# A graph-network layer on Trainium2: TensorE's sums moved one quarter earlier, VectorE's additions moved to the head of a group, the maximum taken on VectorE, the end reordered

## The chip, the cores and the metric

One core of one Trainium2 chip runs the kernel. The metric is the device time of one execution in microseconds (us). The kernel before took 2541.52 us, the median of 3 runs (2540.87 to 2542.66). The execution that was profiled took 2545.81 us by its own time and has a span of 2544.0 us.

## The reference

The layer works on a graph with 6250 nodes (64 numbers each) and 206250 edges (32 numbers each), sorted by the node they end in (`dst`).

```python
h = jnp.maximum(_layernorm(x, axis=-1), 0.0)
msg_in = jnp.concatenate([h[src], h[dst], edge_attr_32], axis=-1)
messages = act(msg_in @ W1 + b1) @ W2 + b2            # act = swish
att_logits = act(msg_in @ Wa1 + ba1) @ Wa2 + ba2
att = jax.nn.softmax(att_logits, axis=0)              # over all edges
aggregated = jax.ops.segment_sum(messages * att, dst, num_segments=6250)
upd_in = jnp.concatenate([h, aggregated], axis=-1)
out = x + act(upd_in @ Wu1 + bu1) @ Wu2 + bu2
```

All of it is float32. Each edge needs one row that depends on its source, one that depends on its destination, and its own features, through two small layers; then a softmax over all edges, and a sum by destination.

## The kernel before

A first stage (about 100 us) normalises x and writes two tables to HBM: `p_tab` with h @ [W1, Wa1] for sources and `q_tab` with the same for destinations, 128 numbers a node.

The main stage goes through 81 groups of 20 tiles of 128 edges (the last, LAST = 80, has 12). A quarter is 4 tiles; a full group has NQ = 5 of them, one PSUM bank (`ps_z[q]`, 128x512) each. All loops over groups are written out in full, so each engine has one long fixed order of instructions, and engines meet only at semaphores.

For group g and quarter q:

- GpSimd (`gather`, L388 to L397) fetches the source rows of each tile from `p_tab` with one indirect DMA of 64 KB (128 rows of 512 bytes) into `p_rows[:, a, ...]`, where a = g % 2. So a quarter's place in `p_rows` is free for group g when VectorE has added the same quarter of group g - 2: `pool.wait_ge(z_ok, (g - 2) * NQ + q + 1)`.
- ScalarE (`one_hot_abs`, `one_hot_relu`) makes the one-hot matrix of the destinations in `comb`, from `dst_b`, which SyncE loads (`load_dst_b`, 960 KB a group). SyncE also loads the edge features into `comb` (`load_ef`) and the window of `q_tab` (`load_window`), when `z_done` says that TensorE has read the group that had that place.
- TensorE (`zmm`, L604 to L615) computes z, the sum before the first activation without the source part, for group g + 1 while VectorE works on group g, and counts `z_done` once a quarter. In the trace each float32 matmul stands as two instructions, so a quarter is 8 of them (128x128).
- VectorE (`add_rows`, L893 to L897) adds the gathered source rows to the quarter in PSUM, and counts `z_ok`. ScalarE (L516) applies Silu into `s2` and counts `silu_ok`, which also frees the bank for the next z.
- VectorE (`logits`, L884 and L886) forms the attention logits, L944 and L946 add the bias and take the largest of each lane. TensorE turns that column into a row (`column_max`, L633), VectorE takes the largest (`group_max`, L904), TensorE spreads it to all lanes (`spread_max`, L638), and VectorE (`running_max`, L915) writes `neg_max`.
- ScalarE (`weights`, L504 and L506) takes the exponentials, VectorE (`one_hots` L861, `weighted` L890 and L891) makes `hot` and `v`, TensorE (`sums`, L617 to L625) sums v by destination into `ps_part` with 20 matmuls (40 instructions, 128x96), and counts `part_done`. VectorE (`add_part`, L869 to L876) loads the window's first node into a register, waits for `part_done` and adds the sums to `acc`; then it updates `ref` and `zp`.

The order inside one group g on TensorE is `column_max(g-1)`, z quarter 0 of g + 1, `spread_max(g-1)`, z quarters 1 and 2, `sums(g-1)`, z quarters 3 and 4. On VectorE it is: the additions of quarters 1 to 4 of group g between the other steps, then L944 and L946, then quarter 0 of group g + 1, then `add_part(g-1)`:

```python
if nxt is not None:
    add_rows(nxt, 1 - a, 0)
if late:
    add_part(g - 1, 1 - a)
```

The end (from L986 on) takes the last maximum, the last weights and sums, adds them, reads a flag and branches on it (a general path that isn't taken here), and computes the update of all nodes in 7 blocks (`rescale`, `aggregate`, `own_part`, `new_rows`, `whole_y`).

## Time and profile before

| what | value |
|---|---|
| median of 3 runs | 2541.52 us |
| the profiled execution, own time | 2545.81 us |
| its span | 2544.0 us |
| GpSimd busy | 1529.6 us, 60% of the span, 1628 instructions |
| TensorE matmuls busy | 1335.2 us, 52%, 7010 instructions |
| VectorE busy | 953.6 us, 37%, 1722 instructions |
| ScalarE busy | 925.1 us, 36%, 1106 instructions |
| mean granted TensorE clock | 0.653 |
| DMA | 228.42 MB, mean 90 GB/s |

Busy time is the time with an instruction at work. "Idle before" in a row is the time that the engine stood still before the instruction, and the name behind the arrow is what ended it, as the semaphores' records tell: "issue" means that nothing recorded ended it, "remote" that the semaphore's releaser on this core had been done long before. Matmul records can be missing here and there.

### The profile page before, as it was taken

Reading aid. Unit: us, or ns where it says so; the run is one execution under the profiler, and the core shown is the slowest. Engines: PE = TensorE matmul, PEld = TensorE weight load, DVE = VectorE, ACT = ScalarE, POOL = GpSimd, SP = SyncE. Lnnn points to the kernel's source line nnn. Section 1 sums busy time; section 2 is a strip of 40 time slices with the busy share of each in tenths; the row PEclk is TensorE's granted clock in tenths of the full one; section 3 lists DMA queues with packets and bytes.
Section 4 is the critical chain, followed back from the end, with each engine's and each line's share of the span. In section 5 each row is a group of like instructions: output and inputs, shape, how many; then the busy total and the mean of one; then the engine's idle time right before and its main releaser. Section 6 shows DMA issues by size and latency. Waiting matters only on the chain.

```text
span 2544.0 us, 20784 instructions
## 1 busy us (share of the span) xinstructions
PE 1335.2 (52%) x7010; PEld 1126.5 (44%) x7010; DVE 953.6 (37%) x1722; ACT 925.1 (36%) x1106; POOL 1529.6 (60%) x1628
## 2 busy tenths in 40 slices
PE   5245555555455555555455555555555455555556
PEld 3234444444444444444444444444444444444444
DVE  4234334433333333433333333333333333443345
ACT  3333333433333333343333333343333333333333
POOL 3665656666666656666666666666666665666650
PEclk8666666666766666666766666666766666666667
DMA  7433333333333333333333333333333333333321
GB/s 193 105 88 84 88 85 91 87 88 92 97 88 87 87 85 90 88 88 89 98 90 88 87 86 89 89 87 87 97 93 88 88 87 85 91 87 87 95 67 27
DMA packets 101988, 228.42 MB, mean 90 GB/s; under 512 B 45185, under 2 KB 65461, under 8 KB 91637
## 3 DMA queue, kind: packets, MB, share of 16 engines
q1 hardware_dynamic: 47588, 120.63, 18.2%
q0 software_dynamic: 51584, 105.75, 16.3%
q8 instruction: 58, 0.95, 0.2%
q10 hardware_dynamic: 2704, 0.66, 0.1%
q14 instruction: 54, 0.43, 0.1%
HBM read 218.91 MB, written 8.00 MB: 89 GB/s over the span
## 4 chain that ended last, share of the span: by engine, by line
another core or an unknown queue 53%; ACT 17%; DVE 14%; issue 11%; PE 3%; DVEq 1%; ACTq 0%; SPq 0%; DMA 0%
ACT s L516 5%; DVE bank L897 5%; ACT L516 4%; ACT comb L484 3%; DVE prod L884 3%; ACT comb L490 3%; DVE lg L886 3%; PE bank L624 1%; ACT bank L504 1%; PE bank L613 1%; DVE lgb L944 1%; PE bank L575 1%; DVE gmax L904 1%; ACT fade L506 1%
## 5 line engine op out<-in xcount | busy, mean ns | idle before, releaser
L396 POOL DMA_INDIRECT p_rows<-p_tab,src_all x1612 | 1521.6, 944 | 943.7 <-issue 466.9
L613 PE MATMUL bank<-q_win,comb 128*128 128x128 f32 x3224 | 825.6, 385 | 842.6 <-issue 832.1
L613 PEld LDWEIGHTS bank<-q_win,comb 128*128 128x128 f32 x3224 | 669.0, 279 | 952.2 <-issue 950.9
L516 ACT ACTIVATE s<-bank 128x512 f32<-128x512 f32 x403 | 239.0, 594 | 1434.4 <-DVE bank L897 1424.7
L874 DVE SCALAR_TENSOR_TENSOR acc<-acc,fade,bank 65x96 f32 x80 | 24.8, 310 | 1330.3 <-remote 1326.7
L624 PE MATMUL bank<-hot,v 128*65 128x96 f32 x3224 | 393.7, 300 | 165.2 <-issue 149.7
L624 PEld LDWEIGHTS bank<-hot,v 128*65 128x65 f32 x3224 | 378.4, 180 | 186.0 <-issue 169.0
L897 DVE TENSOR_TENSOR bank<-bank,p_rows 128x512 f32<-128x512 f32 x403 | 277.0, 688 | 15.7 <-issue 15.7
L484 ACT ACTIVATE comb<-dst_b,row_of 96x1024 f32<-96x1024 int32 (+1 forms) x162 | 217.8, 1345 | 55.3 <-DMA dst_b<-dst_row 55.3
L490 ACT ACTIVATE comb<-comb,ones 96x1024 f32<-96x1024 f32 (+1 forms) x162 | 218.8, 1351 | 2.7
L861 DVE TENSOR_TENSOR hot<-bank,rel 128x960 f32<-128x960 f32 x162 | 185.1, 1143 | 0.0
L884 DVE TENSOR_TENSOR prod<-s,bank 128x512 f32<-128x512 f32 (+2 forms) x163 | 130.9, 803 | 134.4 <-ACT s L516 128.3
L886 DVE TENSOR_REDUCE lg<-prod 128x8 f32<-128x512 f32 (+2 forms) x163 | 132.4, 812 | 5.6
L504 ACT ACT_TABLE_LOAD x81 | 103.9, 1283 | 75.7 <-issue 64.4
L891 DVE TENSOR_TENSOR v<-s,bank 128x1300 f32<-128x1300 f32 x80 | 119.9, 1499 | 0.0
L516 ACT ACT_TABLE_LOAD x81 | 103.9, 1283 | 1.4
L633 PE MATMUL bank<-ident,pmax 128*1 128x128 f32 x81 | 29.8, 368 | 99.7 <-issue 96.7
L638 PE MATMUL bank<-gmax,ones 1*128 1x1 f32 x162 | 46.7, 355 | 42.2 <-DVE gmax L904 41.2
L638 PEld LDWEIGHTS bank<-gmax,ones 1*128 1x128 f32 x162 | 39.8, 303 | 64.6 <-DVE gmax L904 64.5
L633 PEld LDWEIGHTS bank<-ident,pmax 128*1 128x1 f32 x81 | 6.4, 79 | 135.3 <-issue 131.5
L904 DVE TENSOR_REDUCE gmax<-bank 1x1 f32<-1x128 f32 x81 | 21.8, 269 | 16.8 <-remote 16.3
L504 ACT ACTIVATE bank<-lgb,neg_max 128x20 f32<-128x20 f32 (+1 forms) x81 | 22.7, 281 | 1.0
(107 smaller groups left out, 321.0 us busy)
## 6 DMA issues: line engine op xcount, KB each, us to landing
dst_b<-dst_row SPq DMA_DIRECT2D x80, 960.0 KB
p_rows<-p_tab,src_all POOLq DMA_INDIRECT x1612
comb<-efT SPq DMA_DIRECT2D x80, 320.0 KB
q_win<-q_tab SPq DMA_DIRECT2D x81, 48.0 KB
p_tab<-s SPq DMA_DIRECT2D x12, 256.0 KB
q_tab<-s SPq DMA_DIRECT2D x12, 256.0 KB
out<-s SPq DMA_DIRECT2D x6, 256.0 KB, 2.3
x_sb<-x SPq DMA_DIRECT2D x2, 512.0 KB, 5.0
```

The costliest lines, as they stand in the source:

```text
L396: pool.indirect_dma_start(p_rows[:, a, t * H2:(t + 1) * H2], None, p_tab, bass.IndirectOffsetOnAxis(src_all[:, g * TG + t:g * TG + t + 1], ...
L484: nc.scalar.activation(comb[0:WIN, a, c0:c1], dst_b[:, c0:c1], ACT.Abs, bias=row_of[0:WIN, bass.ds(g, 1)]).then_inc(abs_ok, 1)
L490: nc.scalar.activation(comb[0:WIN, a, c0:c1], comb[0:WIN, a, c0:c1], ACT.Relu, scale=-1.0, bias=ones[0:WIN, 0:1]).then_inc(comb_ok, 1)
L504: nc.scalar.activation(ps_w[:, 0:tiles(g)], lgb[:, 0:tiles(g)], ACT.Exp, bias=nm).then_inc(w_ok, 1)
L516: nc.scalar.activation(silu_rows(a, q), halves(ps_z[q][:]), ACT.Silu).then_inc(silu_ok, 1)
L613: last = nc.tensor.matmul(ps_z[q][:, (t % TQ) * H2:(t % TQ + 1) * H2], comb[:, a, t * P:(t + 1) * P], q_win[:, a, :], start=True, stop=True)
L624: last = nc.tensor.matmul(ps_part[0:U1, 0:WIN], v[:, t, :], hot[:, t * WIN:(t + 1) * WIN], start=(t == 0), stop=(t == T - 1))
L861: nc.vector.tensor_tensor(hot[:, t0 * WIN:(t0 + n) * WIN].rearrange("p (t n) -> p t n", t=n), iota_c[:, 0:WIN].unsqueeze(1).broadcast_to([ ...
L884: nc.vector.tensor_tensor(prod[:, 0:t1 - t0], att, wa2c.unsqueeze(1).broadcast_to([P, t1 - t0, U]), ALU.mult).then_inc(s_sem, 1)
L886: nc.vector.tensor_reduce(lg[:, t0:t1], prod[:, 0:t1 - t0], AX.X, ALU.add).then_inc(s_sem, 1)
L891: return nc.vector.tensor_tensor(v[:, 0:T, :], s2[:, ab, 0:T, 0:U1], ps_w[:, 0:T].unsqueeze(2).broadcast_to([P, T, U1]), ALU.mult)
L897: nc.vector.tensor_tensor(ps_z[q][:], ps_z[q][:], p_rows[:, a, q * 512:(q + 1) * 512], ALU.add).then_inc(z_ok, 1)
```

## The change

- GpSimd's `gather` waits, for quarter 2, first for a new semaphore `tile_ok` (one tile's place is free), issues one gather, and waits for the rest of the quarter before the second.
- `add_rows` adds quarter 2 in two instructions, 128x128 and 128x384, and counts `tile_ok` after the first.
- On VectorE, a group begins with the additions of its quarters 0, 1 and 2, with short steps of the group before in between; the additions of quarters 3 and 4 follow the maximum and the first logits; `add_part` of group g - 2, the one-hots and the weighting of g - 1 stand at the group's end.
- The maximum over lanes no longer goes through TensorE: the biased logits of 4 blocks of 32 lanes are written side by side on 32 lanes (`biased`), reduced (`lane_max`), transposed on VectorE and reduced again (`spread_max`), and written to the 4 blocks of `neg_max`.
- On TensorE, `sums(g-1)` stands behind z quarters 0 and 1 of group g + 1, and quarters 2, 3 and 4 behind it; `column_max` and `spread_max` are gone. The one transpose that they did for the flag in group 1 goes into `sums`.
- At the end: ScalarE runs one Exp on a dummy before the last weights; VectorE makes v before it sums the weights; the wait for the last sums and the last addition to `acc` come behind the branch; five of the seven `own_part` products stand ahead of the last sums, each in a bank of its own.

```diff
@@ gpsimd, gather
-                    if not (isinstance(g, int) and g < 2):
-                        pool.wait_ge(z_ok, (g - 2) * NQ + q + 1)
+                    if g > 1:
+                        if q == 2:
+                            pool.wait_ge(tile_ok, g - 1)
+                        else:
+                            pool.wait_ge(z_ok, (g - 2) * NQ + q + 1)
                     for t in range(q * TQ, (q + 1) * TQ):
+                        if g > 1 and t == 2 * TQ + 1:
+                            pool.wait_ge(z_ok, (g - 2) * NQ + q + 1)
@@ scalar
             groups(act, group)
+            nc.scalar.activation(rz[:], ones[:, 0:1], ACT.Exp)
             weights(LAST, 0)
@@ tensor, group
-                if late:
-                    column_max(g - 1)
                 for q in [q for q in (0,) if q in quarters]:
                     zmm(nxt, 1 - a, q)
-                if late:
-                    spread_max(g - 1)
-                for q in [q for q in (1, 2) if q in quarters]:
+                for q in [q for q in (1,) if q in quarters]:
                     zmm(nxt, 1 - a, q)
                 if late:
                     sums(g - 1)
-                for q in [q for q in (3, 4) if q in quarters]:
+                for q in [q for q in (2, 3, 4) if q in quarters]:
                     zmm(nxt, 1 - a, q)
@@ tensor, end
             own_part(0)
             own_part(1)
-            column_max(LAST)
-            spread_max(LAST)
-            pe.wait_ge(zp_ok, 1)
             pe.wait_ge(silu_ok, LAST * NQ + TL // TQ)
-            nc.tensor.matmul(ps_zall, ones[:], zp[:], start=True, stop=True).then_inc(zall_done, 1)
-            sums(LAST)
+            for b in range(2, 5):
+                own_part(b)
...
@@ vector, add_rows
-                nc.vector.tensor_tensor(ps_z[q][:], ps_z[q][:], p_rows[:, a, q * 512:(q + 1) * 512], ALU.add).then_inc(z_ok, 1)
+                n = 0
+                if q == 2:
+                    n = H2
+                    nc.vector.tensor_tensor(ps_z[q][:, 0:n], ps_z[q][:, 0:n], p_rows[:, a, q * 512:q * 512 + n], ALU.add).then_inc(tile_ok, 1)
+                nc.vector.tensor_tensor(ps_z[q][:, n:], ps_z[q][:, n:], p_rows[:, a, q * 512 + n:(q + 1) * 512], ALU.add).then_inc(z_ok, 1)
@@ vector, group (new)
+                late = g > 0
+                add_rows(g, a, 0)
+                if late:
+                    logits(1 - a, 2, NQ, silu_ok, g * NQ, s_ok, g * 4 - 2)
+                add_rows(g, a, 1)
+                if late:
+                    biased(g - 1)
+                add_rows(g, a, 2)
+                if late:
+                    lane_max(g - 1)
+                    spread_max(g - 1)
+                    running_max(g - 1)
+                logits(a, 0, 2, silu_ok, g * NQ + 2, s_ok, g * 4)
+                if g < LAST - 1:
+                    add_rows(g, a, 3)
+                    add_rows(g, a, 4)
+                if g > 1:
+                    add_part(g - 2, a)
+                if late:
+                    one_hots(g - 1, 0)
+                    one_hots(g - 1, 1)
+                    weighted(g - 1, 1 - a)
...
@@ vector, end
-            dve.wait_ge(part_done, NG)
-            win = acc[:, bass.ds(node, WIN)]
-            nc.vector.scalar_tensor_tensor(win, win, fade[0:U1, 0:1], ps_part[0:U1, 0:WIN], ALU.mult, ALU.add).then_inc(acc_ok, 1)
-            dve.wait_ge(acc_ok, NG)
 
             misfit = dve.value_load(flag[0:1, 0:1], min_val=0, max_val=1)
...
+            dve.wait_ge(part_done, NG)
+            win = acc[:, bass.ds(node, WIN)]
+            nc.vector.scalar_tensor_tensor(win, win, fade[0:U1, 0:1], ps_part[0:U1, 0:WIN], ALU.mult, ALU.add).then_inc(acc_ok, 1)
+            dve.wait_ge(acc_ok, NG)
```

What this makes of the written-out orders follows for two engines. On TensorE, one group in the middle of the program, before (the z matmuls are L613, the sums L624):

```order
L633 MATMUL bank<-ident,pmax 1x128
L613 MATMUL bank<-q_win,comb 128x128 x4
L638 MATMUL bank<-gmax,ones 128x1
L613 MATMUL bank<-q_win,comb 128x128 x8
L624 MATMUL bank<-hot,v 65x96 x20
L613 MATMUL bank<-q_win,comb 128x128 x8
```

and now (z is L622, the sums L636):

```order
L636 MATMUL bank<-hot,v 65x96 x20
L622 MATMUL bank<-q_win,comb 128x128 x20
L636 MATMUL bank<-hot,v 65x96 x20
L622 MATMUL bank<-q_win,comb 128x128 x20
```

Of the next group's 20 z matmuls, 12 stood ahead of the sums and 8 behind them; now 8 stand ahead and 12 (quarters 2, 3 and 4) behind. The two small products for the maximum are gone.

On VectorE, before, from the last step of a group's logits to the second addition of the next (L897 are additions of z, L874 the addition of the sums):

```order
L886 TENSOR_REDUCE lg<-prod 128x12
L944 TENSOR_SCALAR lgb<-lg,ba2c 128x20
L946 TENSOR_REDUCE pmax<-lgb 128x1
L897 TENSOR_TENSOR bank<-bank,p_rows 128x512
L871 TENSOR_LOAD base_i
L871 ISA x2
L874 ISA
L874 SCALAR_TENSOR_TENSOR acc<-acc,fade,bank 65x96
L867 REGISTER_ALU
L867 TENSOR_SCALAR ref<-ones,neg_max 65x96
L876 SCALAR_TENSOR_TENSOR zp<-zp,fade,wsum 128x1
L897 TENSOR_TENSOR bank<-bank,p_rows 128x512
```

and now the head of a group, up to its fourth addition (L911 and L912 are additions of z):

```order
L912 TENSOR_TENSOR bank0<-bank0,p_rows 128x512
L895 TENSOR_TENSOR prod<-s2,bank7 128x768
L897 TENSOR_REDUCE lg<-prod 128x12
L912 TENSOR_TENSOR bank1<-bank1,p_rows 128x512
L918 TENSOR_SCALAR lgb<-lg,ba2c 128x20
L921 TENSOR_SCALAR lgb<-lg,ba2c 32x20 x3
L911 TENSOR_TENSOR bank2<-bank2,p_rows 128x128
L912 TENSOR_TENSOR bank2<-bank2,p_rows 128x384
L927 TENSOR_REDUCE qmax<-lgb 32x1
L932 STREAM_TRANSPOSE qmaxB<-qmax 32x32
L934 TENSOR_REDUCE top<-qmaxB 32x1
```

No wait for the sums (L871, L874) stands between the additions of quarters 0, 1 and 2 any more; it comes behind all five.

## Rows read from the trace of the kernel before

**Rows 1.** Page, three groups; list of waits: engine, line, releaser: us, times, longest.

```profile
L396 POOL DMA_INDIRECT p_rows<-p_tab,src_all x1612 | 1521.6, 944 | 943.7 <-issue 466.9
...
L861 DVE TENSOR_TENSOR hot<-bank,rel 128x960 f32<-128x960 f32 x162 | 185.1, 1143 | 0.0
...
L891 DVE TENSOR_TENSOR v<-s,bank 128x1300 f32<-128x1300 f32 x80 | 119.9, 1499 | 0.0
...
DVE acc L874 <- remote: 1326.7, 77, 17.4
...
POOL p_rows L396 <- issue: 466.9, 1532, 0.3
POOL p_rows L396 <- DVE bank L897: 439.6, 79, 8.9
```

**Rows 2.** Timeline of one group: start us, duration, engine, line, [idle before].

```profile
1227.38 0.94 POOL L396 DMA_INDIRECT p_rows<-p_tab,src_all  x1 [5.41 <-DVE bank L897]
...
1233.55 3.52 PE L624 MATMUL bank<-hot,v 128*65 128x96 f32 x40 [1.91 <-issue]
...
1237.64 0.23 DVE L944 TENSOR_SCALAR lgb<-lg,ba2c 128x20 f32<-128x20 f32 x1
...
1251.11 0.94 POOL L396 DMA_INDIRECT p_rows<-p_tab,src_all  x1 [0.30 <-issue]
...
1256.00 0.31 DVE L874 SCALAR_TENSOR_TENSOR acc<-acc,fade,bank 65x96 f32 x1 [17.31 <-remote]
1256.06 0.31 SPq L276 DMA_DIRECT2D comb<-efT  x1
...
1256.54 0.69 DVE L897 TENSOR_TENSOR bank<-bank,p_rows 128x512 f32<-128x512 f32 x1
...
1257.50 0.94 POOL L396 DMA_INDIRECT p_rows<-p_tab,src_all  x1 [5.45 <-DVE bank L897]
```

**Rows 3.** Timeline of TensorE's matmuls in the same group.

```profile
1236.90 0.75 PE L613 MATMUL bank<-q_win,comb 128*128 128x128 f32 x5
...
1241.00 0.37 PE L613 MATMUL bank<-q_win,comb 128*128 128x128 f32 x1 [0.47 <-issue]
1241.69 0.37 PE L613 MATMUL bank<-q_win,comb 128*128 128x128 f32 x1 [0.33 <-issue]
...
1255.77 1.44 PE L613 MATMUL bank<-q_win,comb 128*128 128x128 f32 x6 [0.33 <-issue]
```

**Rows 4.** Timeline of the first groups: the gathers that end GpSimd's stops.

```profile
103.76 0.94 POOL L396 DMA_INDIRECT p_rows<-p_tab,src_all  x1 [7.38 <-DVE bank L897]
143.91 0.94 POOL L396 DMA_INDIRECT p_rows<-p_tab,src_all  x1 [5.50 <-DVE bank L897]
168.34 0.94 POOL L396 DMA_INDIRECT p_rows<-p_tab,src_all  x1 [4.76 <-DVE bank L897]
```

**Rows 5.** Timeline of the first groups: VectorE after long waits, and one burst of sums.

```profile
142.76 0.28 DVE L904 TENSOR_REDUCE gmax<-bank 1x1 f32<-1x128 f32 x1 [16.26 <-remote]
...
149.30 5.33 PE L624 MATMUL bank<-hot,v 128*65 128x96 f32 x40 [1.91 <-issue]
...
166.84 0.31 DVE L874 SCALAR_TENSOR_TENSOR acc<-acc,fade,bank 65x96 f32 x1 [12.43 <-remote]
```

**Rows 6.** Timeline where the gathers end: the last gather, the last sums beside it, VectorE.

```profile
2470.55 5.24 PE L624 MATMUL bank<-hot,v 128*65 128x96 f32 x40 [1.91 <-issue]
...
2473.12 0.95 POOL L396 DMA_INDIRECT p_rows<-p_tab,src_all  x1 [0.30 <-issue]
...
2476.21 0.31 DVE L874 SCALAR_TENSOR_TENSOR acc<-acc,fade,bank 65x96 f32 x1 [0.52 <-PE bank L624]
```

**Rows 7.** Timeline: a 128x128 addition in the first stage; two places of the program's end.

```profile
77.33 0.29 DVE L795 TENSOR_TENSOR s<-bank,b_q 128x128 f32<-128x128 f32 x1 [4.87 <-issue]
...
2506.26 1.28 ACT L504 ACT_TABLE_LOAD   x1 [3.08 <-DVE neg_max L915]
...
2517.82 3.49 DVE L1079 TENSOR_TENSOR acc<-acc,ref 65x1024 f32<-65x1024 f32 x3 [3.63 <-issue]
```

More of the change, by code:

```diff
@@ L666, in _ @@
             own_part(1)
-            column_max(LAST)
-            spread_max(LAST)
-            pe.wait_ge(zp_ok, 1)
             pe.wait_ge(silu_ok, LAST * NQ + TL // TQ)
-            nc.tensor.matmul(ps_zall, ones[:], zp[:], start=True, stop=True).then_inc(zall_done, 1)
-            sums(LAST)
+            for b in range(2, 5):
+                own_part(b)
+            pe.wait_ge(acc_ok, LAST)
+            pe.wait_ge(v_ok, NG)
+            for t in range(TL):
+                if t in (0, TL // 2):
+                    pe.wait_ge(hot_ok, 2 * LAST + 1 + 2 * t // TL)
+                if t == TL // 2 + 2:
+                    pe.wait_ge(zp_ok, 1)
+                    nc.tensor.matmul(ps_zall, ones[:], zp[:], start=True, stop=True).then_inc(zall_done, 1)
+                last = nc.tensor.matmul(ps_part[0:U1, 0:WIN], v[:, t, :], hot[:, t * WIN:(t + 1) * WIN], start=(t == 0), stop=(t == TL - 1))
+            last.then_inc(part_done, 1)
             pe.wait_ge(flag_ok, 1)
@@ new lines, in running_max @@
+            def running_max(g):
+                dve.wait_ge(top_ok, g + 1)
+                wait(dve, negm_ok, 4 * g)
+                for k in range(4):
+                    nm = neg_max[32 * k:32 * (k + 1), bass.ds(g, 1)]
+                    if g == 0:
+                        nc.vector.tensor_scalar(nm, top[:], -1.0, None, ALU.mult).then_inc(negm_ok, 1)
+                    else:
+                        nc.vector.scalar_tensor_tensor(nm, top[:], -1.0, neg_max[0:32, bass.ds(g - 1, 1)], ALU.mult, ALU.min).then_inc(negm_ok, 1)
```

159 lines of the change are left out of this document (74 added, 85 removed).

## The prediction

> **What bounds the kernel now.** The page comes first: GpSimd has the largest busy share, 1521.6 us in 1612 gathers of 944 ns [rows 1]. The chain of waits is of little use here, since over half of it goes to "another core or an unknown queue". The list of waits tells more: between gathers GpSimd idles 0.30 us each time, and 79 times, 439.6 us in all, it waits for VectorE's addition [rows 1]. VectorE itself waits 1326.7 us in 77 pieces before the addition of the sums (L874), with "remote" as the releaser [rows 1].
>
> The timeline of one group shows how these hang together [rows 2]. GpSimd starts at 1227.38 and issues 20 gathers, the last at 1251.11: 23.73 us for 19 steps, 1.25 us each, and it ends at 1252.05. Then it lacks the place of a quarter 1. That addition (L897 at 1256.54) stands behind `add_part` in VectorE's order, and `add_part` waits from 1238.69 to 1256.00. GpSimd goes on at 1257.50. The group takes 30.12 us, 25.0 of gathers and 5.1 of stop.
>
> Why does `add_part` wait until 1256.00? By its records TensorE ended the sums at 1237.07 [rows 2]. But SyncE, which waits for another TensorE count (`z_done`), is released at 1256.06, in the same moment. And TensorE, with nothing to wait for, is slow in just this stretch: after a first quick run the matmuls come at 0.70 us steps, until at 1255.77 six run in 1.44 us [rows 3]. I read this so: **while gathers run, TensorE's counts are held back once some number of its matmuls have been issued, and they all come out a few us after the last gather.** The first groups bear it out. With 28 gathers (103.76 to 138.41) VectorE's wait for the maximum, also a TensorE count but with no register load ahead of it, ends at 142.76, 4.35 us after GpSimd's stop; with 16 gathers (143.91 to 163.58) L874 starts 3.26 us after it [rows 4, 5]; with 20 it is 3.95 us [rows 2]. Where gathers end at 2474.07 for good, L874 waits only 0.52 us and starts at 2476.21, with the sums over at 2475.79 [rows 6]. So GpSimd and VectorE wait for each other: the count comes only when GpSimd stands, and GpSimd stands until VectorE has the count.
>
> **The change part by part.** The stop is made of three pieces [rows 2]: 3.95 us from the last gather's end to VectorE's release, 1.23 us of VectorE (L874, two short steps, the 128x512 addition, 1256.00 to 1257.23), and 0.27 us to GpSimd's start, 5.45 us in all.
>
> *Where the stop lies now.* VectorE adds quarters 0 and 1 of a group before it needs a late TensorE count; quarter 2 stands behind 40 instructions of sums and 8 of z on TensorE. The sums began 6.2 us after GpSimd's start (1233.55); now a second addition (0.69), `add_part`'s own steps (0.54) and the maximum on VectorE (some 1.3) stand ahead of them too, so they begin at about 8.7 us. The count of quarter 2 is then given at about 15 us, later than that of the sums before (9.7 us), and is held back just the same. I expect one stop per group, again after 20 gathers, at `tile_ok`.
>
> *The second piece.* It becomes one addition of 128x128 from PSUM, 0.29 us by the nearest row [rows 7]. That is 0.94 us less. The other part of quarter 2 (about 0.56 us) is done before the first gather of 1.25 us ends, so it costs GpSimd nothing, and neither does `add_part`, which now stands behind all five additions.
>
> *The first piece.* Measured: 3.26, 3.95 and 4.35 us, longer with more gathers. What counts may be the gathers since the stop, which stay 20 (then 3.95 us), or the time since the burst of TensorE work began. That burst begins at 8.7 us, not at 6.2, which brings it from 18.5 to 16.0 us before the last gather's end; in the 16-gather stop it was 14.3 us (from 149.30) [rows 5]. By a line through 14.3 and 18.5 the piece would be 3.5 us. I take the middle, 3.7 us. The ends for the range are no gain here, and 0.7 us (the 3.26 of the row).
>
> *The third piece* stays. New stop: 3.7 + 0.29 + 0.27 = 4.26 us, against 5.45: 1.19 us a group, times 78 of the 79 stops (the first is a matter of the start): **93 us**.
>
> *What is hidden.* The maximum on VectorE adds three bias instructions, a second reduction, a transpose and three writes, some 10 instructions of 0.15 to 0.24 us, 1.5 us, less L904. VectorE is busy 37% and waits 17 us a group, so this costs nothing; if that cover were gone it would be 1.3 us x 80, 104 us. TensorE loses two small products; it too has slack. What is late next? After the release TensorE must have quarters 3 and 4 soon. Behind the sums (8.7 to about 14 us) it has 24 instructions, 7 quick ones and 17 at 0.70 us [rows 3], so it ends near 27 us, before the release at 28.4.
>
> The Trainium skill, page SBUF — State Buffer, section Who interferes with whom, says that a VectorE `tensor_scalar` in a 2-port mode locks GpSimd out of a shared port, so that it can't write descriptors. The trace shows no sign of it: L944 of 0.23 us at 1237.64 lies beside gathers that keep their mean of 944 ns [rows 1, 2]. By the page alone three more such instructions would cost up to 0.7 us a group, 55 us in all; the sum above goes by the row.
>
> *The end.* The Exp table is loaded ahead (1.28 us). The branch, 3.63 us of "issue" before L1079, now runs beside the last sums instead of behind them. These two give 4.9 us [rows 7]. Three products leave the path of the first blocks; they may lie beside other work, so I count them as 0 at the low end and as another 6 us at the high one (a choice, without a row), and take **8 us** in all.
>
> *Sum.* 93 + 8 = 101 us, from 2545.8 us, the profiled execution's own time: 2444.8. The median lies 4.3 us lower, so 2440.5; I say **2441 us**, 4% faster.
>
> **The rivals.**
>
> *No stop at all.* If TensorE's count had another cause for its lateness, or came in time because fewer instructions lie ahead of it (48 since the stretch's start instead of some 60), GpSimd would never wait: 25.0 us a group, 78 x 5.1 + 8 = 406 us less, 2135 us. The Trainium skill, page TensorE: Matmul & The Clock Gate, section The cost: per-tile semaphore tail, has a count out within tens of ns of its matmul; by that rule the hold is none of TensorE's, and this is the case that follows. Against it are the three waits that end together with GpSimd's stop [rows 2, 5].
>
> *The gain of VectorE's second piece is taken back by the first*: if the release depends on the work since the last one and not on GpSimd's stop, the later sums push it out by the 1 us that was won. Only the end's gain stays, 2533 us, or none of it, 2541.
>
> *Slower.* What waits before L874 may not be the count but the register load of `add_part` (L871 in the order), held by the gathers. Then VectorE, which now loads behind its five additions, would stand there until GpSimd stops, and GpSimd would stop for a quarter 0 instead: its release then comes after `add_part` (0.54), one-hots (2 x 1.14), weighting (1.5) [rows 1] and an addition (0.69): 3.95 + 5.0 + 0.27 = 9.2 us, 3.8 more than now, 78 x 3.8 - 8 = 288 us slower, 2830 us. It decides from the point where the load itself takes over about 10 us. Against it: L904 at 142.76 waited 16.26 us with no load ahead of it, and SyncE has none at all [rows 2, 5].
>
> **How the numbers follow.** My forecast, one shorter stop a group, has 0.80. No stop has 0.06, the gain taken back 0.06, slower 0.08 (with 0.02 in it for a second stop in a group, if quarters 3 and 4 come too late). The forecast's own range: no gain in the first piece and 4 us at the end gives 0.94 x 78 + 4 = 77, 2464; the full 0.7 and 11 us give 139, 2403. Below and above I add half as much again for a first piece that no row of this order bounds: 2375 to 2500. Outside are the three rivals, 0.20 in all. Measurements of this kernel tell 0.2% (5 us) from no change. Faster by more: 0.80 + 0.06 and half of the gain taken back, 0.88; the same 0.04; slower 0.08.
>
> **What would show it right or wrong.** Right: GpSimd waits some 79 times, for the 128x128 addition (L911), 330 to 350 us in all; the gap before it is 4.0 to 4.6 us; 20 gathers at 1.25 us lie between. VectorE's long wait stands before L911 and is "remote"; `add_part` (L885) waits for nothing. The first piece can be read as the time from the last gather's end to L911's start: 3.95 says that gathers count, 3.5 that the burst counts. Wrong: gaps for L912, two gaps a group, a long wait before L885, gathers over 0.95 us, or no gap at all.

## The result and the profile after

| | kernel before | changed kernel |
|---|---|---|
| median (runs) | 2541.55 us (4) | 2584.09 us (4) |
| lowest, highest | 2540.87, 2542.66 | 2574.86, 2587.07 |
| ratio, 95% interval | | 1.0164 [1.0144, 1.0185] |
| profiled execution | 2545.81 us, span 2544.0 | 2583.27 us, span 2581.6 |

The change makes the kernel 1.6% slower on this chip. The forecast was 4% faster. (The kernel before has one run more here than in the table ahead of the prediction.)

The page of the changed kernel, its busy times and the rows of the main stage, and two lines of its list of waits (us in all, times, longest); they answer to [rows 1]:

```profile
PE 1185.2 (46%) x6767; PEld 1018.0 (39%) x6767; DVE 1073.6 (42%) x2368; ACT 916.6 (36%) x1107; POOL 1529.8 (59%) x1628
...
L404 POOL DMA_INDIRECT p_rows<-p_tab,src_all x1612 | 1522.7, 945 | 978.3 <-DVE bank L911 468.1
...
L911 DVE TENSOR_TENSOR bank<-bank,p_rows 128x128 f32<-128x128 f32 x81 | 24.2, 299 | 1150.9 <-PE bank L622 1150.9
...
DVE bank L911 <- PE bank L622: 1150.9, 78, 16.1
...
POOL p_rows L404 <- DVE bank L911: 468.1, 77, 9.8
```

GpSimd's gathers last as long as before, but its idle time ahead of them grew from 943.7 to 978.3 us. The stops stand where they were forecast, at the 128x128 addition (L911), which takes 299 ns (forecast 0.29). But VectorE's wait before L911 does not end with "remote". It ends with a TensorE matmul of z, L622.

One group on the timeline of the changed kernel (start, duration, engine, line; rows left out; to be read against [rows 2, 3]):

```profile
1214.31 0.94 POOL L404 DMA_INDIRECT p_rows<-p_tab,src_all  x1 [6.36 <-DVE bank L911]
...
1222.64 4.22 PE L636 MATMUL bank<-hot,v 128*65 128x96 f32 x29 [4.33 <-DVE v L902]
...
1227.15 0.24 PE L636 MATMUL bank<-hot,v 128*65 128x96 f32 x1 [0.29 <-issue]
...
1228.58 0.70 DVE L912 TENSOR_TENSOR bank<-bank,p_rows 128x512 f32<-128x512 f32 x1 [3.54 <-remote]
...
1238.04 0.94 POOL L404 DMA_INDIRECT p_rows<-p_tab,src_all  x1 [0.30 <-issue]
1238.45 0.32 PE L636 MATMUL bank<-hot,v 128*65 128x96 f32 x1 [1.11 <-issue]
1240.58 0.32 PE L636 MATMUL bank<-hot,v 128*65 128x96 f32 x1 [1.81 <-issue]
1241.28 0.32 PE L636 MATMUL bank<-hot,v 128*65 128x96 f32 x1 [0.39 <-issue]
1241.98 0.32 PE L636 MATMUL bank<-hot,v 128*65 128x96 f32 x1 [0.38 <-issue]
1242.68 3.58 PE L622 MATMUL bank<-q_win,comb 128*128 128x128 f32 x16 [0.38 <-issue]
1244.58 0.30 DVE L911 TENSOR_TENSOR bank<-bank,p_rows 128x128 f32<-128x128 f32 x1 [14.35 <-PE bank L622]
...
1245.15 0.94 POOL L404 DMA_INDIRECT p_rows<-p_tab,src_all  x1 [6.18 <-DVE bank L911]
```

GpSimd starts at 1214.31, its 20th gather begins at 1238.04 and ends at 1238.98. TensorE turns quick again at 1242.68, 3.70 us later: that is the release, as late as before. But TensorE has not run one instruction of quarter 2 by then. It ran 29 instructions of the sums quickly, and the last 11 one by one, from 1227.15 to 1241.98. Quarter 2 comes only now, and VectorE can start its addition 1.90 us after the release. So the stop is 3.70 + 1.90 + 0.57 = 6.17 us here, on the mean of 80 stops 5.95 us, where it was 5.56 us over 79 before. All stops together are 36 us longer, of the 37.6 us by which the span grew.

Two readings fall with these rows. At the slow pace a matmul takes not one step of 0.70 us but two, as the weight load ahead of it takes one as well: the 11 slow matmuls start within 14.83 us, some 1.4 to 1.5 us apart on the mean, though their steps are uneven. And the quick run ends in the middle of the sums, not behind them.

### The profile page after: what moved, and what is told of

It reads as the page before. It is cut to its first block, busy times and chain, and to the rows that moved or that the text cites. A ratio compares the mean times of both kernels' runs of the same rounds, so it can differ in the third digit from the quotient of the medians.

```text
span 2581.6 us, 21023 instructions
## 1 busy us (share of the span) xinstructions
PE 1185.2 (46%) x6767; PEld 1018.0 (39%) x6767; DVE 1073.6 (42%) x2368; ACT 916.6 (36%) x1107; POOL 1529.8 (59%) x1628
## 4 chain that ended last, share of the span: by engine, by line
issue 47%; PE 31%; DVE 18%; DVEq 2%; another core or an unknown queue 1%; ACTq 0%; DMA 0%; ACT 0%
PE bank L636 22%; PE bank L622 8%; DVE hot L865 5%; DVE prod L895 2%; DVE bank L912 2%; DVE v L902 2%; DVE neg_max L945 1%; DVEq L875 1%; DVE bank L911 1%; DVE acc L885 1%; DVE ref L871 1%; DVE qmaxB L932 1%; DVE top L934 1%; PE bank L732 0%
## 5 line engine op out<-in xcount | busy, mean ns | idle before, releaser
L404 POOL DMA_INDIRECT p_rows<-p_tab,src_all x1612 | 1522.7, 945 | 978.3 <-DVE bank L911 468.1
L636 PE MATMUL bank<-hot,v 128*65 128x96 f32 x3200 | 576.0, 322 | 1256.4 <-issue 1089.7
L636 PEld LDWEIGHTS bank<-hot,v 128*65 128x65 f32 x3200 | 452.4, 193 | 1338.0 <-issue 1164.2
L622 PE MATMUL bank<-q_win,comb 128*128 128x128 f32 x3224 | 549.1, 342 | 86.9 <-issue 74.0
L622 PEld LDWEIGHTS bank<-q_win,comb 128*128 128x128 f32 x3224 | 526.9, 255 | 149.1 <-issue 148.2
L911 DVE TENSOR_TENSOR bank<-bank,p_rows 128x128 f32<-128x128 f32 x81 | 24.2, 299 | 1150.9 <-PE bank L622 1150.9
L912 DVE TENSOR_TENSOR bank<-bank,p_rows 128x512 f32<-128x512 f32 (+1 forms) x403 | 260.4, 665 | 258.9 <-remote 227.1
L897 DVE TENSOR_REDUCE lg<-prod 128x8 f32<-128x512 f32 (+1 forms) x162 | 132.2, 816 | 5.5
L895 DVE TENSOR_TENSOR prod<-s,bank 128x512 f32<-128x512 f32 (+1 forms) x162 | 131.4, 811 | 3.9 <-ACT s L524 1.3
L921 DVE TENSOR_SCALAR lgb<-lg,ba2c 32x20 f32<-32x20 f32 (+1 forms) x243 | 60.6, 249 | 7.8
L945 DVE SCALAR_TENSOR_TENSOR neg_max<-top,neg_max 32x1 f32<-32x1 f32 x320 | 48.1, 150 | 10.6 <-DVE top L934 0.3
L871 DVE TENSOR_SCALAR ref<-ones,neg_max 65x96 f32 x81 | 35.7, 441 | 0.0
L885 DVE SCALAR_TENSOR_TENSOR acc<-acc,fade,bank 65x96 f32 x80 | 24.2, 302 | 0.1
```

Of the source, the lines that this page charges most:

```text
L404: pool.indirect_dma_start(p_rows[:, a, t * H2:(t + 1) * H2], None, p_tab, bass.IndirectOffsetOnAxis(src_all[:, g * TG + t:g * TG + t + 1], ...
L622: last = nc.tensor.matmul(ps_z[q][:, (t % TQ) * H2:(t % TQ + 1) * H2], comb[:, a, t * P:(t + 1) * P], q_win[:, a, :], start=True, stop=True)
L636: last = nc.tensor.matmul(ps_part[0:U1, 0:WIN], v[:, t, :], hot[:, t * WIN:(t + 1) * WIN], start=(t == 0), stop=(t == T - 1))
L895: nc.vector.tensor_tensor(prod[:, 0:t1 - t0], att, wa2c.unsqueeze(1).broadcast_to([P, t1 - t0, U]), ALU.mult).then_inc(s_sem, 1)
L897: nc.vector.tensor_reduce(lg[:, t0:t1], prod[:, 0:t1 - t0], AX.X, ALU.add).then_inc(s_sem, 1)
L912: nc.vector.tensor_tensor(ps_z[q][:, n:], ps_z[q][:, n:], p_rows[:, a, q * 512 + n:(q + 1) * 512], ALU.add).then_inc(z_ok, 1)
```

## The experiments

Two words in this part: a "row" is one matmul instruction on TensorE, of which each group has 80 (40 of z, 8 a quarter, and 40 of the sums); "rows left" is the number of z rows that TensorE runs between the release and the next sums. At 32 left quarter 2 is just done, at 40 it is not begun.

The experiments ran in five sets, each on one chip with the kernel before beside it. The kernel before took 2523.5, 2108.5, 2105.1, 2525.3 and 2524.6 us in them. Ratios are to the kernel before of the same set. The changed kernel itself was run again in the second, third and fourth set, not in the first and fifth.

### First set: the kernel before takes 2523.46 us (2520.55 to 2526.88)

**Quarter 2 ahead of the sums again**, all else as changed.

```diff
-                for q in [q for q in (1,) if q in quarters]:
+                for q in [q for q in (1, 2) if q in quarters]:
                     zmm(nxt, 1 - a, q)
                 if late:
                     sums(g - 1)
-                for q in [q for q in (2, 3, 4) if q in quarters]:
+                for q in [q for q in (3, 4) if q in quarters]:
```

> The changed kernel with TensorE's sums behind quarters 0, 1 and 2 of the next z again, as before; all else as changed. Theory A (quarter not reached): at the release TensorE has not yet run the matmuls behind the slow sums, so the first quarter behind them costs its 8 matmuls, some 1.8 us, after the release. Now quarter 2 runs ahead of the sums, so if VectorE stops at it, the stop falls to 3.95 + 0.30 + 0.27 = 4.5 us and the time to 2581.6 - 77 x 1.5, about 2465 us. If its count comes before GpSimd stops, VectorE stops at quarter 3 instead, which lies behind the sums: 3.95 + 1.8 + 0.69 + 0.27 = 6.7 us, about 2635 us. Theory B (the release itself comes later or VectorE's own steps cost): the place of the sums does not matter, 2570 to 2595 us with the wait still before the 128x128 addition.

Measured: 2477.98 us, ratio 0.9823 [0.9789, 0.9857]. Mean stop 4.57 us. One stop of the same version, from its run in the fourth set:

```profile
1202.28 1.30 DVE L912 TENSOR_TENSOR bank<-bank,p_rows 128x512 f32<-128x512 f32 x2 [16.11 <-remote]
...
1203.24 0.94 POOL L404 DMA_INDIRECT p_rows<-p_tab,src_all  x1 [4.61 <-DVE bank L912]
```

The stop now stands at quarter 3, added whole. For that case I had expected 6.7 us and 2635 us: I took quarter 3's matmuls to be undone at the release. They are done: in 72 of 79 groups all 40 rows of the sums are quick, and in most only 19 to 22 z rows are left, none of them of quarter 3.

**Quarter 2 added whole**, in the changed order: `add_rows` without its first instruction of 128x128, `gather` without `tile_ok`.

> The changed kernel without the split of quarter 2: one addition of 128x512, and GpSimd waits for it. Theory A and B alike: the piece between release and GpSimd's start grows by 0.69 - 0.30 = 0.39 us less what the shorter list of instructions gives, 77 x 0.35 = 27 us, about 2611 us. If the split itself cost something on VectorE or GpSimd, it would be less than 2600 us.

Measured: 2485.69 us, ratio 0.9853 [0.9815, 0.9892], against 2611 us expected. Mean stop 4.79 us. One group of its timeline (L631 the sums, L617 z, L904 the addition):

```profile
1205.84 6.20 PE L631 MATMUL bank<-hot,v 128*65 128x96 f32 x40 [3.82 <-DVE v L897]
...
1226.19 4.25 PE L617 MATMUL bank<-q_win,comb 128*128 128x128 f32 x27 [0.33 <-issue]
1226.44 0.70 DVE L904 TENSOR_TENSOR bank<-bank,p_rows 128x512 f32<-128x512 f32 x1 [16.69 <-remote]
...
1227.41 0.94 POOL L399 DMA_INDIRECT p_rows<-p_tab,src_all  x1 [4.79 <-DVE bank L904]
```

All 40 rows of the sums are quick here, quarter 2 fits into the slow stretch, and VectorE's wait ends "remote": at the release, not at a matmul. (Over the whole execution 47 of these waits end "remote" and 34 at a matmul of L617.) A split addition should be 0.4 us better than a whole one. It isn't where TensorE is late: the changed kernel, run in the fourth set, has a ratio of 0.995 and a mean stop of 5.13 us. The two versions were not run in one set with stops.

**Half of the sums' matmuls left out.**

```diff
-                for t in range(T):
-                    last = nc.tensor.matmul(..., start=(t == 0), stop=(t == T - 1))
+                for t in range(0, T, 2):
+                    last = nc.tensor.matmul(..., start=(t == 0), stop=(t == T - 2))
```

> The changed kernel with every second tile left out of the sums (10 matmuls for 20 in each full group), so the aggregated sums lack half of the edges. Theory A: TensorE has 20 instruction pairs fewer in the slow stretch and reaches quarter 2 before the release; stop 4.2 to 4.5 us, GpSimd still stops once a group, 2581.6 - 77 x 1.5 to 1.8, 2445 to 2470 us. Theory B: unchanged or nearly so, 2570 to 2585 us, with the wait before the 128x128 addition ended at 3.95 + 1.8 us after the last gather.

Measured: 2428.6 us, ratio 0.9627 [0.9580, 0.9674], below the 2445 to 2470 us expected. Its waits and one stop:

```profile
DVE bank L911 <- remote: 1224.3, 78, 21.4
...
POOL p_rows L404 <- DVE bank L911: 321.9, 78, 7.2
```

```profile
1226.20 0.30 DVE L911 TENSOR_TENSOR bank<-bank,p_rows 128x128 f32<-128x128 f32 x1 [15.65 <-remote]
...
1226.77 0.94 POOL L404 DMA_INDIRECT p_rows<-p_tab,src_all  x1 [3.99 <-DVE bank L911]
```

This is the stop that was forecast: 4.13 us on the mean (forecast 4.26), VectorE released by the count itself. What stood between the forecast and the result is TensorE's work ahead of quarter 2.

**`dst_b` loaded in group 0 only** (later groups load 4 numbers, so their one-hot matrices are wrong).

> The changed kernel in which SyncE loads dst_b (960 KB a group) for the first group alone and 4 numbers a row for the others, so the one-hots are wrong. If TensorE is slowed by the gathers alone (theories A and B), nothing changes: 2575 to 2590 us. If the big load is what fills the DMA engines and holds TensorE back, the slow stretch goes: no stop or a short one, 2150 to 2450 us.

Measured: 2506.62 us, ratio 0.9937 [0.9913, 0.9960], mean stop 4.97 us, TensorE's slow stretch as before. The changed kernel, run in another set, gave 0.995. So the load of 960 KB a group makes neither the slow stretch nor the stop. The 2575 to 2590 us expected were a figure of the first chip.

### Second set: the kernel before takes 2108.53 us (2102.93 to 2112.26)

The kernel before and the changed kernel, on another chip, take 17 to 19% less. The changed kernel, unaltered:

> The changed kernel, unaltered, once more beside the kernel before. In the first experiments the kernel before took 2523.5 us, not 2541.6, and the changed kernel without its split 2485.7. If the split is what makes the changed kernel slow, this run takes about 2584 us (ratio 1.016). If that first set's chip runs differently, and the change stands near a threshold (whether TensorE has run quarter 2 at the release), it takes less than the run with the whole quarter: stops of about 4.5 us, 2455 to 2475 us, ratio 0.975.

Measured: 2105.21 us, ratio 0.9987 [0.9972, 1.0003], which neither expectation had. The kernel before, profiled once:

> The kernel before, unaltered, for a profile beside that of the run above. The stop of GpSimd should be 5.2 to 5.5 us; L874 starts 3.7 to 3.95 us after the last gather. If the release came earlier here by what the time differs (18 us over 78 groups, 0.23 us), that is the first piece of the stop.

Measured: 2109.49 us, and none of the stops that I expected. The waits of the changed kernel here:

```profile
DVE bank L912 <- DMA p_rows<-p_tab,src_all: 725.9, 212, 5.8
POOL p_rows L404 <- issue: 484.8, 1591, 0.3
DVE bank L911 <- DMA p_rows<-p_tab,src_all: 153.1, 69, 4.1
```

GpSimd never stops. It issues 1612 gathers, one each 1.25 us, 2012 us, and VectorE waits for their data. TensorE has no slow stretch. The change then has nothing to act on in the main stage. So the rival "no stop" described a real execution (2135 us was its time), but of both kernels.

**Half of the gathers left out** from group 2 on (the other half of each quarter keeps old rows):

> The changed kernel with every second tile's gather left out from group 2 on, so half of the source rows are stale: 10 gathers a group, one TensorE load as before. Theory A (TensorE gets one instruction each 0.70 us while gathers run, past the first 60 or 100): with half of the gathers the slow stretch is at most 12.5 us long and most of TensorE's work is done without it; group time falls well below 25 us, to 16 to 20 us, limited by VectorE (13 us busy) and the chain through the weights: 1450 to 1800 us. If TensorE's slowness has nothing to do with the gathers, the groups stay at 25 us or more, over 2100 us.

Measured: 1355.18 us, ratio 0.6428 [0.6388, 0.6468], faster than either reading. **Plain DMAs** of the same size instead of the indirect ones (each tile fetches fixed rows):

> The changed kernel with a plain DMA of 128 rows of 512 bytes from a fixed place in the table for each indirect gather, issued by GpSimd in the same order and with the same waits, so the source rows are wrong. If the indirect gather as such (1.25 us of GpSimd each) is the load that slows TensorE, the slow stretch goes or changes; if any DMA issued by GpSimd does it, the 0.70 us steps stay. Issue time of a plain DMA is not known from any row: 0.5 to 1.5 us; so 1500 to 2700 us, and the steps are what is to be read.

Measured: 1352.71 us, ratio 0.6416 [0.6390, 0.6442]; a plain DMA keeps GpSimd 535 ns, an indirect one 945. Both versions end at the same time, and in both GpSimd now waits for VectorE's additions. So in this state the gathers' pace is worth 750 us; no other edit tried in it moved the time by more than 0.15%. Without a slow stretch these two versions can't tell what makes it, which is what they were built for.

### Third set: the kernel before takes 2105.11 us (2100.52 to 2110.99)

Four kernels were to be compared where there are stops; this set had none either. The last of them is the kernel before with a single edit, the sums behind quarters 0 and 1 (`(1, 2)` becomes `(1,)`, and `(3, 4)` becomes `(2, 3, 4)`).

> The changed kernel, nothing altered, beside three versions on one chip. There are two kinds of chip so far: with stops of GpSimd in every group (kernel before 2541 and 2523 us) and without any (2108 us). Theory A (TensorE's order is what costs: the sums' last eleven rows stand in the slow stretch and quarter 2 behind them): where the chip has stops the ratio to the kernel before is again near 1.016 and over 1.01. Theory B (the loss belongs to the first chip, and a chip of the second kind with a kernel before of 2523 gives a gain as the whole-quarter version did, 0.985): ratio 0.98 to 0.99. On a chip without stops both say 0.998 to 1.001.

> The changed kernel with TensorE running quarter 2 of the next z ahead of the sums, as before the change, and all else changed. Theory A: with stops, 0.98 to 0.985 of the kernel before (2478 of 2523 on another chip), and over 2% under the changed kernel of this chip. Theory B: the changed kernel within 0.5% of it. Without stops: 0.998 to 1.001, GpSimd's gathers set the time.

> The changed kernel with quarter 2 added whole: GpSimd's first gather of that quarter waits for all four tiles. My steps of the prediction say slower than the changed kernel by about one addition a group, 0.3 us x 78 = some 25 us. Theory C (the split costs: it frees one gather early, which starts the stretch in which counts are late before the rest is ready): with stops 0.985 of the kernel before and 3% under the changed kernel. Theory A without C: within 1.5% of the changed kernel, so over 1.005 of the kernel before. Without stops: 0.998 to 1.001.

> The kernel before with one edit of the change alone: TensorE does the sums behind quarters 0 and 1 of the next z, not behind three. Theory A: with stops, later restarts in each group, 2 to 4% slower than the kernel before (50 to 100 us over 78 groups). My prediction's own reasons: faster, since the addition of quarter 2 would no longer be kept by TensorE's queue order; that reading expects 0.97 to 1.0. Without stops: 0.998 to 1.001.

Measured: 1.0004 [0.9990, 1.0018], 1.0005 [0.9991, 1.0020], 1.0002 [0.9986, 1.0017] and 1.0015 [1.0003, 1.0027]. Without stops TensorE's order makes no difference over 0.15%.

### Fourth set: the kernel before takes 2525.27 us (2519.91 to 2529.30)

> The changed kernel again, hoping for a chip with GpSimd's stops (kernel before over 2400 us; of four chips so far two had them, two not). Theory A (TensorE's order costs): ratio over 1.01. Theory B (the loss belongs to the first chip alone): 0.98 to 0.99. Without stops: 0.998 to 1.001, the period of a group 20 x 1.25 = 25 us on GpSimd.

> The changed kernel with quarter 2 of the next z ahead of the sums. With stops: 0.98 to 0.985 of the kernel before. Theory A: over 2% faster than the changed kernel of this chip; Theory B: within 0.5% of it. Without stops: 0.998 to 1.001.

> The kernel before with the sums behind two quarters of the next z, nothing else. Theory A: with stops 1.02 to 1.04; my prediction's reading: 0.97 to 1.0. Without stops 0.999 to 1.002 (1.0015 was seen).

Measured: the changed kernel 2513.39 us, ratio 0.9950 [0.9930, 0.9969]; three quarters ahead of the sums 2479.80 us, 0.9811 [0.9778, 0.9845]; the kernel before with two quarters 2525.50 us, 1.0003 [0.9992, 1.0015].

Neither theory had this. Put behind two quarters in the kernel before, the sums cost nothing (I expected 2 to 4%): there GpSimd waits for the sums' count (L874) anyhow, as the list of waits of that run shows, and all 40 rows are quick in 76 of 78 groups.

```profile
DVE acc L874 <- remote: 1284.0, 76, 17.2
```

In the changed kernel, which waits for quarter 2, the same place costs 1.4%. And the changed kernel itself is 0.5% faster here where it was 1.6% slower on the first chip. Its timeline shows why:

```profile
1209.83 5.93 PE L622 MATMUL bank<-q_win,comb 128*128 128x128 f32 x33 [0.33 <-issue]
...
1210.24 0.30 DVE L911 TENSOR_TENSOR bank<-bank,p_rows 128x128 f32<-128x128 f32 x1 [16.10 <-PE bank L622]
...
1210.81 0.94 POOL L404 DMA_INDIRECT p_rows<-p_tab,src_all  x1 [4.45 <-DVE bank L911]
...
1219.15 3.02 PE L636 MATMUL bank<-hot,v 128*65 128x96 f32 x34 [3.38 <-issue]
```

At the release 33 rows are left here, not 40, and the quick run is cut after 34 rows of the sums, not after 29. Counting the rows left in each group of both timelines gives (the release is read from the first quick matmul, so a count can be off by one):

| rows left | changed kernel, first chip: mean stop (groups) | fourth set |
|---|---|---|
| up to 32 | | 4.41 us (7) |
| 33, 34 | | 4.74 us (22) |
| 35, 36 | 5.75 us (2) | 5.16 us (22) |
| 37, 38 | 5.87 us (33) | 5.47 us (23) |
| 39, 40 | 6.14 us (27) | |

Each row left costs 0.15 to 0.2 us. The first chip's execution stood at 37 to 40 in 60 of these 62 groups, the fourth set's between 31 and 38. The stops differ by 0.8 us, 64 us over 78, of the 71 us between 2584 and 2513. The rows make up some 0.6 us of that. The other 0.2 us is the release itself: with 37 or 38 rows left it comes 3.70 us after the last gather's end on the first chip and 3.51 us in the fourth set. The kernel before shows this too: its L874 starts 3.84 us after the last gather's end on the first chip, and 3.60 us in the fourth set's version with the sums behind two quarters, which takes as long as the kernel before of that set (medians of 79 and 78 stops). Over 78 groups that is 19 us, as much as the 16 us between 2541.5 and 2525.3. Why the release comes later on the first chip is open.

### Fifth set: the kernel before takes 2524.56 us (2516.76 to 2526.29)

**The sums begin sooner**: VectorE's steps `ref` and `zp` move from in front of the one-hots to behind the weighting.

```diff
                 if g > 1:
-                    add_part(g - 2, a)
+                    node = add_part(g - 2, a, rest=False)
                 if late:
                     one_hots(g - 1, 0)
                     one_hots(g - 1, 1)
                     weighted(g - 1, 1 - a)
+                if g > 1:
+                    part_rest(g - 2, a, node)
```

> The changed kernel with VectorE's two short steps ref (L871) and zp (L887) moved from in front of the one-hots to behind the weighting, so that TensorE's sums begin some 0.7 us sooner in a group. Corrected theory: TensorE runs quickly until some 12 to 13 us after GpSimd's restart and then only 13 matmul rows until GpSimd has stopped; what it has ahead of quarter 2's count at that point is paid for in the stop. In the changed kernel (stops of 5.13 us) 11 rows of sums and the 8 of quarter 2 stand there. 0.7 us more hold eight more rows, so nearly all 40 sums run quickly, quarter 2 fits into the slow rows, its count is out at the release, and VectorE's addition starts 3.5 to 3.8 us after the last gather: stop 4.1 to 4.4 us, 0.75 to 1.0 us less, 60 to 80 us over 78 groups; ratio to the kernel before 0.963 to 0.975. Rival (the stop is set by GpSimd's count of gathers and by the release alone, the rows don't matter): stop as in the changed kernel, ratio 0.995. On a chip or in a call without stops: 0.999 to 1.001.

Measured: 2496.41 us, ratio 0.9901 [0.9878, 0.9923], mean stop 4.75 us, where 4.1 to 4.4 us and 0.963 to 0.975 were expected. Against the changed kernel of the fourth set (5.13 us) the stop fell by 0.4 us, about half of what was expected. The rival (rows don't matter, ratio 0.995) fails as well. An early group, and one of the late ones:

```profile
257.59 5.49 PE L622 MATMUL bank<-q_win,comb 128*128 128x128 f32 x24 [0.33 <-issue]
...
266.42 5.17 PE L636 MATMUL bank<-hot,v 128*65 128x96 f32 x40 [3.34 <-issue]
...
2058.21 5.65 PE L622 MATMUL bank<-q_win,comb 128*128 128x128 f32 x33 [0.32 <-issue]
...
2067.22 2.94 PE L636 MATMUL bank<-hot,v 128*65 128x96 f32 x33 [3.36 <-issue]
```

```profile
258.39 0.95 POOL L404 DMA_INDIRECT p_rows<-p_tab,src_all  x1 [4.29 <-DVE bank L917]
...
1230.65 0.95 POOL L404 DMA_INDIRECT p_rows<-p_tab,src_all  x1 [5.27 <-DVE bank L917]
...
2059.18 0.94 POOL L404 DMA_INDIRECT p_rows<-p_tab,src_all  x1 [4.39 <-DVE bank L917]
```

In the early groups the expectation holds: 24 rows left, all 40 rows of the sums quick, a stop of 4.29 us. Then the place slides, 24, 26, 27 and on to 32 to 38, and stays there. By rows left the means are 4.27 us (up to 32), 4.63, 5.10 and 5.40 (37, 38): the table of the fourth set again, in another kernel. So the price of a row shows in three executions.

What cuts the quick run isn't a time after GpSimd's start, as I had expected. The sums begin 0.3 us sooner in this kernel (8.03 us after the start, median of 60 groups, against 8.34) and are still cut after 33 rows. Nor does the quick run end at one time after the start in the other versions: its end lies 8.7 us behind it with three quarters ahead of the sums (fourth set), 12.7 us in the changed kernel beside it, and 13.7 us with quarter 2 whole (medians). I read it as a balance: a group has 80 rows, the slow stretch takes 10 to 14 of them in most groups (12 or 13 in the middle; 15 in the kernel before with two quarters), so about 68 run quickly between two stretches, whatever they are. Where the slow stretch lies among the 80 is then set by where it lay in the group before, and only the stop's own length pulls at it. That would explain how one kernel can run at 33 or at 38 rows left. It was not tested by itself, and what fixes the 12 rows is open.

**The split moved to quarter 3**, in the old TensorE order. There quarter 3 is the one behind the sums, and the one that GpSimd waits for.

```diff
@@ on top of the first experiment's edit
-                        if q == 2:
+                        if q == 3:
                             pool.wait_ge(tile_ok, g - 1)
...
-                        if g > 1 and t == 2 * TQ + 1:
+                        if g > 1 and t == 3 * TQ + 1:
...
-                if q == 2:
+                if q == 3:
                     n = H2
```

> TensorE's order as before the change (quarters 0, 1, 2, sums, 3, 4), and the split addition moved from quarter 2 to quarter 3, the one that GpSimd waits for in this order. Corrected theory: the addition that releases GpSimd is 128x128 and not 128x512, 0.4 us less than the 4.70 us of the three-quarter version, whose 13 slow rows hold quarter 3 already: stop 4.25 to 4.35 us, 28 to 35 us under 0.981 of the kernel before, so 0.967 to 0.971. Rival (release and addition overlap somehow, or a fifth quarter becomes the stop): 0.98 or more. Without stops: 0.999 to 1.001.

Measured: 2450.18 us (2449.05 to 2453.75), ratio 0.9712 [0.9691, 0.9733]. A group of its timeline:

```profile
1218.48 5.27 PE L622 MATMUL bank<-q_win,comb 128*128 128x128 f32 x25 [1.02 <-issue]
1218.72 0.30 DVE L911 TENSOR_TENSOR bank<-bank,p_rows 128x128 f32<-128x128 f32 x1 [15.99 <-remote]
...
1219.29 0.94 POOL L404 DMA_INDIRECT p_rows<-p_tab,src_all  x1 [4.32 <-DVE bank L911]
```

The expectation was 0.967 to 0.971 and stops of 4.25 to 4.35 us; the time is at the upper end of it, and the stops before L911 are nearly all 4.0 to 4.4 us. In some 20 groups GpSimd also idles 0.70 us instead of 0.30 behind the first gather, 8 us in all, which I hadn't counted; what it waits for there should be the 128x384 addition, but no record names it. In this order the z rows left at the release are 16 to 25 in nearly all groups, all of other quarters, so no matmul stands ahead of the count. This version is the fastest with full sums where there are stops, 2.9% ahead of the kernel before.

## Why the prediction was wrong

**Where the stop lies: right.** One stop a group, after 20 gathers, at `tile_ok`: 77 of 80 in the trace.

**The first piece: right in its kind, up to 0.25 us short, and not the whole of it.** I took 3.7 us for the time from the last gather's end to VectorE, between "gathers count" (3.95) and "the burst counts" (3.5). Read from TensorE's rows, the release comes 3.7 to 3.8 us after the last gather's end in the changed kernel and in the kernel before (medians of all groups): the later burst moved nothing, and of my two readings "gathers count" is the right one. VectorE starts up to 0.25 us behind the release even where its count is ready. In the sets it is 3.4 to 3.8 us.

**The step that failed** is the sentence "Behind the sums (8.7 to about 14 us) it has 24 instructions, 7 quick ones and 17 at 0.70 us [rows 3], so it ends near 27 us, before the release at 28.4." It is wrong three times, and so is what it leans on, that the count of quarter 2 is given at about 15 us. A matmul at this pace takes two steps of 0.70 us, for its weight load and itself, so 17 of them take 24 us. The sums don't run quickly to their end: 29 or 30 rows do in most groups, and 10 or 11 don't. And what the slow stretch holds is some 12 of the 80 rows, so a step that puts 40 rows ahead of what GpSimd waits for must be read against those. In the timeline shown, quarter 2's matmuls begin 28.4 us after GpSimd's start, at the release, where I had them done by 15 us. The trace before had it [rows 2, 3]: behind 40 quick rows of the sums came 5 quick and then 13 slow rows of z, 11 of quarters 3 and 4 and 2 of the quarter behind them, for which nobody waited yet. Moving quarter 2 behind the sums moved it into these. The price by the trace: 5.95 instead of 4.26 us a stop, 78 times, 132 us.

**The second and third piece: right.** 0.30 and 0.27 us.

**What is hidden: right, as far as the runs show.** VectorE's ten extra instructions cost nothing that can be seen, though no run takes them out alone. Its busy time rose by 120 us. By the Trainium skill, page SBUF — State Buffer, section Who interferes with whom, the three extra `tensor_scalar` instructions would lock GpSimd out if they ran in a 2-port mode; no run shows in which mode they ran. The gathers keep 945 ns, 944 before [rows 1].

**The end: half of the gain is there, and the clock takes it back.** I took 8 us. From the last gather's end to the end of the span it is 72.8 us in the changed kernel and 70.0 in the kernel before; in the second set, where no stop disturbs the place, 47.2 and 47.8. In the second set, VectorE's last addition to `acc`, the product behind it and TensorE's first products of the update, of the changed kernel; then the latter two of the kernel before:

```profile
2072.72 0.31 DVE L1106 SCALAR_TENSOR_TENSOR acc<-acc,fade,bank 65x96 f32 x1 [1.08 <-issue]
2073.06 3.49 DVE L1113 TENSOR_TENSOR acc<-acc,ref 65x1024 f32<-65x1024 f32 x3
...
2076.48 3.68 PE L722 MATMUL bank<-acc,wws 65*64 65x512 f32 x8
```

```profile
2080.96 3.49 DVE L1079 TENSOR_TENSOR acc<-acc,ref 65x1024 f32<-65x1024 f32 x3 [3.83 <-issue]
2082.24 1.98 PE L718 MATMUL bank<-acc,wws 65*64 65x512 f32 x4 [2.52 <-DVE acc L1079]
```

Of the 3.83 us of "issue" 1.08 are left. The first products of the update start 3.5 us sooner, counted from the last gather's end (2057.75 and 2060.01): 18.7 us behind it instead of 22.2. But the last stretch, as the windows view gives it (us, then busy times of the engines, and the granted clock third from the end), runs at another clock. First the changed kernel, then the kernel before:

```profile
2089.00:2105.00 16.00, 12.49 (x43) 7.85 (x42) 4.24 (x7) 1.88 (x4) 0.00 (x0) 0.50 0.31 71
```

```profile
2092.00:2107.80 15.80, 11.78 (x64) 6.63 (x62) 7.82 (x11) 3.11 (x5) 0.00 (x0) 0.93 0.45 103
```

At 0.50 (1.2 GHz) four matmuls of 512 columns take 1.98 us, at 0.93 (nearly 2.4 GHz) 1.08 us. In the kernel before the clock rises in the middle of the seven blocks, in the changed kernel it doesn't. The pair on the first chip shows the same: 0.50 against 0.90 over the last 15 and 17 us. Over the last 15 us it stays at 0.50 in 11 of the 15 profiled runs with the new end, and is 0.95 or 0.96 in all four with the old one. It is 0.96 too in the two versions with half of the gathers or with plain DMAs, so the new end doesn't rule it out. With quarter 2 whole it is 0.61 in the first set, and in the third, the fastest of nine runs, it rose early. That one has 0.98 over its last 12 us, and from the last gather's end to the end 38.8 us, 9.0 less than the kernel before in the second set. That is the size I had forecast, but it is one execution, and the two are of different sets. What makes the clock rise or stay is open.

**The sum.** 2441 us forecast, plus 132 us for the stops, plus 11 us for the end (8 expected, 2.8 lost), is 2584 us. That it meets the median to the microsecond is luck: the forecast took 5.45 us for a stop of before that is 5.56 us on the mean, and stops and end together give 39 us where the spans differ by 37.6.

**The rivals.** None was this one. I asked when the count is let out, and took for granted that there would be one to let out. The rival that ended slower held a register load for the cause; here L885 waits for nothing. The range (2375 to 2500) left the measured time out by 84 us; in the fourth set the same kernel takes 2513 us. The forecast had 0.88 for "faster" where its own parts add up to 0.89.

## What to carry to other kernels

When a wait moves to another count, list what the counting engine has ahead of that count, in instructions, and price each at its pace in that very stretch, not at its pace elsewhere. An order that is free for one waiter (the kernel before) can cost 1.4% for another. And if an engine's slow stretch takes much the same number of a loop's instructions in every version, choose which of them stand there: those that nobody waits for.

## What the runs showed of the hardware

- **Held counts and a paced TensorE are a state of the chip or of the set, not of the kernel.** Every profiled version stops once a group on the first chip and in three sets (kernel before 2541, 2523, 2525, 2525 us); in two sets none that keeps all its indirect gathers stops at all (2108, 2105 us), and the times of the kernel before say the same for all its 40 runs there. The chip numbered 7 in the records gave 2108.5 us in one set and 2525.3 in another, so the number doesn't tell it, if it is the same chip. What sets the state, and what holds the counts, is open. Neither 960 KB less of loads a group nor half as many sums end it. Where there is no hold, counts are quick: in the second set VectorE's L1005 starts at 2071.00, 0.04 us after TensorE's L672 ends (2070.96), which agrees in size with the Trainium skill, page TensorE: Matmul & The Clock Gate, section The cost: per-tile semaphore tail. The Trainium skill, page NOTIFIC — the notification-queue block, section Overflow: three behaviours, one of which stalls the engine, says that a full queue of records can, if it is set up so, stall the engine that makes them. Whether that is the hold seen here was not tried, and no run shows it.
- **Another count is held for only a part of the stretch.** In the timeline above TensorE has done quarter 1 by 1218.3, but VectorE, ready for it at 1225.0, gets its `z_done` only at 1228.58, in the middle of the gathers. Such waits come 76 times on the first chip, 227.1 us, and only 26 times, 48.7 us, in the fourth set. GpSimd doesn't stop for them.
- **An indirect gather of 64 KB keeps GpSimd 945 ns, a plain DMA of 64 KB 535 ns**, in the same place of the same loop (second set).
